# Three edits to a fused adaLN, attention and FFN kernel: VectorE's last residual ahead of the pooling maxima, one activation-table set for Exp and Ln, and the third group's score rows behind half of the next keys

## The chip, the cores and the metric

The kernel runs on one core of a Trainium2 chip. The metric is the device time of one execution in microseconds; each kernel is run several times and the median is taken. The engines of the core are named as in the profile: PE is TensorE's matmul, PEld its weight load, DVE is VectorE, ACT is ScalarE, POOL is GpSimd, and SP is the engine that issues the DMAs.

## What is computed

The input `x` has 64 sequences of 64 tokens with 256 features. Cut to what matters:

```python
def reference(x, ...):
    # rotation of feature halves by an angle and a power that depend on the sequence
    a = amplitudes ** delta_t; ang = frequencies * delta_t
    c, s = a * cos(ang), a * sin(ang)
    xr = [c * x0 - s * x1, s * x0 + c * x1]
    # attention as a decaying recurrence, 16 heads of 16
    q, k, v = split(xr @ W_qkv.T); k = layernorm(k)
    S = sigmoid(log_gamma) * S + v k^T; y = S q
    x = x + y @ W_o.T
    # pooling: scores from tanh, masked softmax over the sequence, divided by a count
    scores = tanh(x @ W1 + b1) @ v
    p = softmax(where(mask, scores, NEG_INF))
    pooled = (p @ x) / cnt
    # FFN with fake quantisation: the scale is the largest |pooled| of the whole tensor
    xq = quant(pooled); h = quant(silu(xq @ Wg.T) * (xq @ Wu.T))
    return x + h @ Wd.T
```

The scale of `quant` needs the maximum over all of `pooled`, so no FFN product can start before the pooling of the last tokens is done.

## The kernel before

The 4096 tokens are worked on in eight groups of 512 (`G = 8`, index `g`). Every engine has its own program, written out by hand in order, and engines meet only at semaphores (`wait_ge`, `then_inc`), so an instruction that waits holds up all that stands behind it on its engine.

**Start.** SP loads the row of parameters. ScalarE makes the decays' logarithm from it (Abs, Exp, Ln: lines 688 to 690) and then the sines (693 to 696, semaphore `trig_ok`). VectorE reduces the angles (1478 to 1486, `ang_ok`), takes the mean of the key weights (1490 and 1491, `mean_ok`), multiplies sines by the powers (1497 and 1498, `cs1_ok`), and rotates group 0 with ScalarE's help (704 on ScalarE, 1505 on VectorE). GpSimd waits for `mean_ok`, centres the key weights (557), copies the other weights (560, 562), makes the remaining powers (543), makes tables (534 to 538, 615, 616), and then rotates group 1 (`rotate`, 575 to 583). GpSimd also makes the low part of every group's turned input (`low_x`, 589, semaphore `xl_ok`).

**A group on TensorE.** Scores of the first half of the heads, values projection (`project_v`), scores of the second half, then for `g` from 2 on the pooling network of group `g - 2` (`hidden_layer`, ScalarE's tanh, `score_rows`), then `values_pair` (the recurrence's values, which wait for VectorE's decays, `dec_done`), and between these the keys and queries of group `g + 1`. A projection of 128 rows is six matmuls of 512 columns; `project_half` issues the first three (step 0: lines 1136 to 1138) or the last three (step 1: 1140, 1142, 1143, of which the last two wait for `xl_ok`). `project_whole` issues both. In groups from 3 on, pooling matmuls stand between `hidden_layer` and `score_rows`; in the third group (`g = 2`) nothing does.

**The last group's tail.** TensorE projects the last output rows (`project`, line 978, `o_mm`), VectorE adds the residual in two halves (`residual(g, 0)` and `residual(g, 1)`, line 1571, `x1_done`), and TensorE's `pool_tokens(G - 1)` (line 1042) waits for both. VectorE further sums the softmax (1657 to 1663) and takes the maxima of group 6's pooled rows (1751, two reductions) and of group 7's (1759, two reductions), then of all (1762, `xm_ok`). TensorE spreads that maximum over the partitions (`every_row`, 1334), behind six matmuls that do no work of the reference (`keep_clock(6, ...)`, 1125), and the quantisation and the FFN follow. ScalarE meanwhile loads the table set for Silu and copies the pooled rows (`pooled_rows(6)`, `last_pooled_rows`, line 788).

Of the kernel before, what the change touches and what calls it, by code (L numbers as in the profile page):

```python
# [7 lines left out]
ALU = mybir.AluOpType  # L8
# [15 lines left out]
DC = D // P  # L24
# [3 lines left out]
PP = 4  # L28
TG = PP * P
G = TOK // TG  # L30
NPAIR = TOK // P
# [30 lines left out]
def build(nc, x, x_t, row, kinds, cols, w_qkv_t, w_o_t, w_o, w1, w_gate, w_up, w_down, out):  # L62
# [7 lines left out]
    with ExitStack() as ctx:  # L70
# [7 lines left out]
        bank = [psum[:, 512 * i:512 * i + 512] for i in range(8)]  # L78
# [124 lines left out]
        a_pow = sb("a_pow", [P, NPAIR])  # L203
        cs = sb("cs", [P, 2, NPAIR])
# [36 lines left out]
        x0_in, cs1_ok, csr_tr, csr_ok = sem("x0_in"), sem("cs1_ok"), sem("csr_tr"), sem("csr_ok")  # L241
# [436 lines left out]
        def _(act):  # L678
# [3 lines left out]
            def link(ins):  # L682
                count[0] += 1
                ins.then_inc(act_c, 1)
                act.wait_ge(act_c, count[0])

            act.wait_ge(ld_row, 16)
            link(act.activation(lg[:, 1, :], lg_raw, ACT.Abs))
            link(act.activation(lg[:, 2, :], lg[:, 1, :], ACT.Exp, scale=-1.0))
# [282 lines left out]
        def _(pe):  # L972
# [61 lines left out]
            def pool_tokens(c):  # L1034
                pe.wait_ge(pT_ok, c + 1)
                for q in range(2):
                    for e in range(2):
                        for b in range(2):
                            rows = slice(S * b, S * b + S)
                            weights = pT[c % 2][rows, q, e * S:e * S + S]  # L1040
                            if c >= TURNED:
                                last = pe.matmul(pool_out(c, q, b)[S * e:S * e + S, :], weights, x1[c % 3][rows, 2 * q + e, :],
                                                 start=True, stop=True)
                                continue
                            for k in range(DC):
                                at_p = k * TG // 2 + (2 * q + e) * S
                                last = pe.matmul(bank[b][:, at_p:at_p + S], x1[c % 3][rows, 2 * q + e, k * P:k * P + P], weights,
                                                 start=True, stop=True)
                    if c == G - 1 or q == 1:
                        last.then_inc(pl_mm, 1)  # L1050
# [159 lines left out]
            for g in range(G):  # L1210
                c = g - 2

                def project_whole(o, s, j, signal):
                    project_half(g + 1, o, s, j, 0, signal)
                    project_half(g + 1, o, s, j, 1, signal)
# [25 lines left out]
                if 3 <= g < G - 1:  # L1241
                    pe.wait_ge(v_ok, PP * g + PP)
                    pool_tokens(c - 1)
                if 2 <= g < G - 1:
                    score_rows(c)
                if g + 1 < G:
# [13 lines left out]
                    if g != 1:  # L1260
                        pe.wait_ge(xT_ok, DC * (g + 1) + DC)
                        pe.wait_ge(v_ok, PP * g + PP)
                        if g >= 3:
                            pe.wait_ge(pl_cp, 2 * c - 1)
                        project_whole(K_BANK, 1, 0, k_mm)
                        if g >= 3:
                            pe.wait_ge(pl_cp, 2 * c)
                        project_whole(K_BANK, 1, 1, k_mm)
# [182 lines left out]
        def _(dve):  # L1451
# [33 lines left out]
            link(dve.tensor_tensor(ang[:, 3, :], ang[:, 3, :], ang[:, 2, :], ALU.min))  # L1485
            dve.tensor_scalar(ang[:, 3, :], ang[:, 3, :], np.pi / 2, None, ALU.add).then_inc(ang_ok, 1)

            dve.wait_ge(ld_k, 16)
            raw_heads = raw_qkv[:, :, D:2 * D].rearrange("p c (h d) -> p c h d", d=DK)
            link(dve.tensor_reduce(mean[:, :, :], raw_heads, AX.X, ALU.add))  # L1490
            dve.tensor_scalar(mean[:, :, :], mean[:, :, :], 1.0 / DK, None, ALU.mult).then_inc(mean_ok, 1)


            first, rest = slice(0, 2 * PP), slice(2 * PP, NPAIR)
            dve.wait_ge(pow_ok, 1)
            dve.wait_ge(trig_ok, 2)
            dve.tensor_tensor(cs[:, 1, first], a_pow[:, first], bank[2][:, first], ALU.mult)
            dve.tensor_tensor(cs[:, 0, first], a_pow[:, first], bank[3][:, first], ALU.mult).then_inc(cs1_ok, 1)
            dve.wait_ge(cs1_ok, 1)
            dve.wait_ge(x0_in, 16)  # L1500
            for h, sign in enumerate((ALU.subtract, ALU.add)):
# [64 lines left out]
            def residual(g, h):  # L1566
                dve.wait_ge(o_mm, 2 * g + h + 1)
                if h == 0:
                    dve.wait_ge(xres_in, 16 * g + 16)
                two = slice(2 * h, 2 * h + 2)  # L1570
                dve.tensor_tensor(x1[g % 3][:, two, :], o_bank(g, h).rearrange("q (p d) -> q p d", p=2), xres[:, two, :],
                                  ALU.add).then_inc(x1_done, 1)
# [82 lines left out]
            def softmax_sums(c):  # L1655
                dve.wait_ge(ex_ok, c + 1)
                dve.tensor_reduce(sm_c[:, 1, :], ex[:, :, :], AX.X, ALU.add).then_inc(cond_c, 1)
# [19 lines left out]
            for g in range(G):  # L1677
# [65 lines left out]
                if g + 1 < G:  # L1743
                    newton(g + 1, 1 if g else None)
                residual(g, 0)
                if g == G - 1:
                    softmax_sums(g)
                    softmax_weights(g)
                    dve.wait_ge(pl_mm, G - 1)
                    for b in range(2):  # L1750
                        dve.tensor_reduce(raw_max[:, 0, :].rearrange("p (q b) -> p b q", b=2)[:, b, :], bank[b].rearrange("p (q d) -> p q d", d=D), AX.X,
                                          ALU.max, apply_absolute_value=True).then_inc(pl_ok, 1)
                residual(g, 1)

            c = G - 1
            for q in range(2):
# [177 lines left out]
```

## Time and profile before

| what | value |
|---|---|
| median of 3 runs | 263.94 us (263.81 to 265.27) |
| the profiled execution's own time | 265.14 us |
| its span in the profile | 263.4 us |
| mean granted TensorE clock | 0.994 of full speed |
| TensorE, VectorE, ScalarE, GpSimd busy | 94%, 84%, 72%, 62% of the span |

All stretches below are read from the one profiled execution, whose own time is 1.74 us more than its span. Times inside it are counted from the span's start. The rows themselves stand in groups further below.

### The profile page before, as it was taken

What the parts mean: (1) busy time and instruction counts of PE and PEld (TensorE: products, weight loads), DVE (VectorE), ACT (ScalarE), POOL (GpSimd) and SP (SyncE); (2) the same over time, 40 slices, a digit from 0 to 9 for tenths busy, and PEclk for the clock granted to TensorE, in tenths of its full rate; (3) what the DMA queues carried; (4) which work ended last, traced back from release to release, by engine and by line L of the source; (5) the groups of instructions that cost most, each with busy time, mean ns of one, the idle gap of its engine ahead of it and who ended that gap; (6) DMA issues with size and microseconds to landing.
All of it is one profiled execution on the core that took longest, in us unless ns stands there. A gap on an engine that the chain in (4) does not pass through costs nothing.

```text
span 263.4 us, 8405 instructions
## 1 busy us (share of the span) xinstructions
PE 247.8 (94%) x3476; PEld 170.4 (65%) x3481; DVE 220.2 (84%) x481; ACT 189.0 (72%) x327; POOL 163.2 (62%) x170
## 2 busy tenths in 40 slices
PE   4999999998999999999999999996899999998994
PEld 4779688696798788789679668765334444443331
DVE  4879679789789889689879849969579999999994
ACT  5895464772796798598694683384699899919990
POOL 6898583796697696694894925240043689730670
PEclk9999999999999999999999999999799999999999
DMA  5991406808607508907906620310056797000367
GB/s 163 341 298 31 150 2 212 113 2 278 122 6 276 124 2 274 188 4 244 207 17 184 121 82 3 113 50 4 0 138 142 129 256 296 0 2 0 118 247 274
DMA packets 42983, 34.34 MB, mean 130 GB/s; under 512 B 25601, under 2 KB 33345, under 8 KB 42945
## 3 DMA queue, kind: packets, MB, share of 16 engines
q1 hardware_dynamic: 42944, 33.80, 47.3%
q8 instruction: 27, 0.44, 0.7%
q14 instruction: 12, 0.09, 0.1%
HBM read 19.48 MB, written 8.42 MB: 106 GB/s over the span
## 4 chain that ended last, share of the span: by engine, by line
PE 71%; DVE 11%; ACT 11%; issue 4%; DMA 1%; POOL 1%; DVEq 0%; ACTq 0%
PE psum L978 17%; PE psum L1017 7%; PE psum L1002 7%; PE psum L1389 6%; PE psum L1136 4%; PE psum L1408 4%; PE psum L1125 3%; DVE arena L1563 3%; PE psum L1142 3%; PE psum L1143 2%; ACT silu L941 2%; PE psum L1140 2%; PE psum L1083 2%; PE psum L1137 2%; PE psum L1138 2%
## 5 line engine op out<-in xcount | busy, mean ns | idle before, releaser
L1563 DVE TENSOR_TENSOR arena<-psum,xq_mem 128x512 f32<-128x512 f32 x64 | 39.7, 683 | 2.2 <-PE psum L1002 2.1
L1389 PE MATMUL psum<-xq_mem,guT 128*128 128x512 bf16 x151 | 33.8, 380 | 0.3
L589 POOL TENSOR_TENSOR xT_lo<-arena,xT 128x512 fp32r<-128x512 f32 x14 | 17.6, 1276 | 16.2 <-ACT xT L739 16.2
L1389 PEld LDWEIGHTS psum<-xq_mem,guT 128*128 128x128 bf16 x152 | 14.4, 98 | 19.3 <-DVE arena L1787 1.8
L1798 DVE TENSOR_REDUCE h_max<-arena 128x1 f32<-128x1024 f32 (+1 forms) x24 | 25.9, 1122 | 0.2
L923 ACT ACTIVATE silu<-psum,gu_x 128x1024 f32<-128x1024 f32 (+1 forms) x24 | 24.4, 1026 | 2.1 <-PE psum L1389 1.1
L721 ACT ACTIVATE arena<-psum,pmask 128x512 f32<-128x512 f32 x32 | 20.2, 686 | 0.8 <-PE psum L1143 0.6
L1017 PE MATMUL psum<-arena 64*32 64x128 f32 x1024 | 19.1, 274 | 1.3 <-DVE arena L1563 1.3
L1408 PE MATMUL psum<-arena,dT 128*128 128x512 bf16 x78 | 18.8, 380 | 1.3 <-DVE arena L1857 0.6
L1002 PE MATMUL psum<-arena 32*64 32x128 f32 x1024 | 19.7, 278 | 0.0
L1017 PEld LDWEIGHTS psum<-arena 64*32 64x32 f32 x1024 | 13.8, 105 | 7.2 <-issue 7.2
L664 POOL CAST arena<-silu 128x1024 bf16<-128x1024 int8 (+1 forms) x9 | 9.6, 1096 | 14.3 <-DVE silu L1852 13.1
L647 POOL CAST arena<-q 128x1024 bf16<-128x1024 int8 x6 | 6.2, 1039 | 18.8 <-ACT q L905 18.8
L575 POOL TENSOR_TENSOR arena<-xin,cs_rows 128x512 f32<-128x512 f32 x7 | 9.0, 1288 | 14.1 <-DMA cs_rows<-cs_dram 14.1
L978 PE MATMUL psum<-wT,xT 128*128 128x256 f32 x64 | 17.5, 295 | 0.0
L1578 DVE SCALAR_TENSOR_TENSOR psum<-psum,pmask,arena 128x256 f32<-128x256 f32 x28 | 12.4, 488 | 6.0 <-ACT arena L728 6.0
L1002 PEld LDWEIGHTS psum<-arena 32*64 32x64 f32 x1024 | 15.6, 130 | 2.7 <-issue 0.5
L978 PE MATMUL psum<-woT,yT 128*128 128x256 f32 x64 | 17.1, 289 | 0.2 <-DVE arena L1652 0.2
L715 ACT ACTIVATE arena<-psum 128x512 f32<-128x512 f32 x16 | 9.6, 599 | 10.5 <-PE psum L1143 10.5
L624 POOL COPY arena<-arena 128x512 uint16<-128x512 uint16 x24 | 16.9, 775 | 0.0
L978 PE MATMUL psum<-wT_lo,xT 128*128 128x256 f32 x64 | 16.7, 283 | 0.0
L978 PE MATMUL psum<-woT_lo,yT 128*128 128x256 f32 x64 | 16.7, 283 | 0.0
(250 smaller groups left out, 725.7 us busy)
## 6 DMA issues: line engine op xcount, KB each, us to landing
arena<-in_x SPq DMA_DIRECT2D x9, 512.0 KB, 4.4
x_dram<-arena SPq DMA_DIRECT2D x8, 512.0 KB, 3.1
pooled<-x_dram SPq DMA_DIRECT2D x8, 512.0 KB, 5.5
out<-pooled SPq DMA_DIRECT2D x15, 256.0 KB, 2.1
xin<-in_x_t SPq DMA_DIRECT2D x7, 512.0 KB, 5.7
cs_rows<-cs_dram SPq DMA_DIRECT2D x12, 256.0 KB, 5.5
pooled<-in_w_qkv_t SPq DMA_DIRECT2D x3, 256.0 KB, 5.3
pooled<-in_w_down SPq DMA_DIRECT2D x1, 704.0 KB, 8.4
```

The source lines that it names most:

```text
L589: pool.tensor_tensor(xT_lo[:, k, :], xrotT[:, k, :], xT[:, k, :].bitcast(F32), ALU.subtract).then_inc(xl_ok, 1)
L624: last = pool.tensor_copy(x1T_words[:, a, h], planesT[:, a, h])
L721: act.activation(qblk[:, c, odd, :], Q_BANK[c][:, :], ACT.Identity, scale=pmask[:, odd:odd + 1]).then_inc(q_ok, 1)
L923: act.activation(silu_tile(n, v)[:, a:], gate_bank(v)[:, a:], ACT.Silu, scale=gu_x[:, 0, v:v + 1]).then_inc(silu_ok, 1)
L978: return pe.matmul(o, w(k), x(k), start=start, stop=stop) if stationary_w else pe.matmul(o, x(k), w(k), start=start, stop=stop)
L1002: mm = pe.matmul(bank[S_BANK[r]][S * b:S * b + S, p * P:p * P + P], kT[rows, c, t:t + S], qblk[rows, c, :, t:t + S], start=True, stop=True)
L1017: last = pe.matmul(Y_BANK[half][b][32 * r:32 * r + 32, at_y:at_y + P], v_rows[rows, p, at_v:at_v + 32], dec[rows, c, r, p, :], start=True, ...
L1389: mm = pe.matmul(in_order(o[:, 512 * half:512 * half + 512], 2 * n + half), gT[i][:, v, c, :], xq_rows(2 * n + half, c), start=(c == 0), s ...
L1408: return pe.matmul(o, dT[:, c, v, :], hid_q[:, U * n + 2 * v + half, 0:512], start=first, stop=last)
L1563: dve.tensor_tensor(dec[:, c, r, :, :], bank[S_BANK[r]].rearrange("q (n k) -> q n k", n=PP), two_heads, ALU.mult).then_inc(dec_done, 1)
L1578: dve.scalar_tensor_tensor(o, y_psum(b, half, 1), pmask[:, 1:2], y_rows(b, half), ALU.mult, ALU.add).then_inc(y_ok, 1)
L1798: dve.tensor_reduce(h_max[:, n, v:v + 1], hid_step(n, v), AX.X, ALU.max, apply_absolute_value=True).then_inc(hm_done, 1)
```

## The change

Four things move. ScalarE is told at its start to load the table set `natural_log_exp_and_others`, which holds Exp and Ln, so no load stands between the two any more. VectorE multiplies the sines before it takes the mean of the key weights. In the third group, TensorE issues the first three matmuls of the next keys ahead of the score rows instead of behind the first `values_pair`. In the last group VectorE adds the second residual right behind the first, then takes group 6's maxima, and only then does the softmax sums.

```diff
--- before.py
+++ after.py
@@ -684,6 +684,7 @@
                 ins.then_inc(act_c, 1)
                 act.wait_ge(act_c, count[0])
 
+            act.preload_act_table_set("natural_log_exp_and_others")
             act.wait_ge(ld_row, 16)
             link(act.activation(lg[:, 1, :], lg_raw, ACT.Abs))
             link(act.activation(lg[:, 2, :], lg[:, 1, :], ACT.Exp, scale=-1.0))
@@ -1241,6 +1242,10 @@
                 if 3 <= g < G - 1:
                     pe.wait_ge(v_ok, PP * g + PP)
                     pool_tokens(c - 1)
+                if g == 2:
+                    pe.wait_ge(xT_ok, DC * (g + 1) + DC)
+                    pe.wait_ge(v_ok, PP * g + PP)
+                    project_half(g + 1, K_BANK, 1, 0, 0, k_mm)
                 if 2 <= g < G - 1:
                     score_rows(c)
                 if g + 1 < G:
@@ -1262,7 +1267,9 @@
                         pe.wait_ge(v_ok, PP * g + PP)
                         if g >= 3:
                             pe.wait_ge(pl_cp, 2 * c - 1)
-                        project_whole(K_BANK, 1, 0, k_mm)
+                        if g != 2:
+                            project_half(g + 1, K_BANK, 1, 0, 0, k_mm)
+                        project_half(g + 1, K_BANK, 1, 0, 1, k_mm)
                         if g >= 3:
                             pe.wait_ge(pl_cp, 2 * c)
                         project_whole(K_BANK, 1, 1, k_mm)
@@ -1485,17 +1492,18 @@
             link(dve.tensor_tensor(ang[:, 3, :], ang[:, 3, :], ang[:, 2, :], ALU.min))
             dve.tensor_scalar(ang[:, 3, :], ang[:, 3, :], np.pi / 2, None, ALU.add).then_inc(ang_ok, 1)
 
-            dve.wait_ge(ld_k, 16)
-            raw_heads = raw_qkv[:, :, D:2 * D].rearrange("p c (h d) -> p c h d", d=DK)
-            link(dve.tensor_reduce(mean[:, :, :], raw_heads, AX.X, ALU.add))
-            dve.tensor_scalar(mean[:, :, :], mean[:, :, :], 1.0 / DK, None, ALU.mult).then_inc(mean_ok, 1)
-
-
             first, rest = slice(0, 2 * PP), slice(2 * PP, NPAIR)
             dve.wait_ge(pow_ok, 1)
             dve.wait_ge(trig_ok, 2)
             dve.tensor_tensor(cs[:, 1, first], a_pow[:, first], bank[2][:, first], ALU.mult)
             dve.tensor_tensor(cs[:, 0, first], a_pow[:, first], bank[3][:, first], ALU.mult).then_inc(cs1_ok, 1)
+
+            dve.wait_ge(ld_k, 16)
+            raw_heads = raw_qkv[:, :, D:2 * D].rearrange("p c (h d) -> p c h d", d=DK)
+            link(dve.tensor_reduce(mean[:, :, :], raw_heads, AX.X, ALU.add))
+            dve.tensor_scalar(mean[:, :, :], mean[:, :, :], 1.0 / DK, None, ALU.mult).then_inc(mean_ok, 1)
+
+
             dve.wait_ge(cs1_ok, 1)
             dve.wait_ge(x0_in, 16)
             for h, sign in enumerate((ALU.subtract, ALU.add)):
@@ -1743,14 +1751,14 @@
                 if g + 1 < G:
                     newton(g + 1, 1 if g else None)
                 residual(g, 0)
+                residual(g, 1)
                 if g == G - 1:
-                    softmax_sums(g)
-                    softmax_weights(g)
                     dve.wait_ge(pl_mm, G - 1)
                     for b in range(2):
                         dve.tensor_reduce(raw_max[:, 0, :].rearrange("p (q b) -> p b q", b=2)[:, b, :], bank[b].rearrange("p (q d) -> p q d", d=D), AX.X,
                                           ALU.max, apply_absolute_value=True).then_inc(pl_ok, 1)
-                residual(g, 1)
+                    softmax_sums(g)
+                    softmax_weights(g)
 
             c = G - 1
             for q in range(2):
```

VectorE's order at the start of the program. `ang` are the angles, `mean` the key weights' means, `cs` the products of power and sine, and `arena` receives the rotated group 0. Before:

```order
L1486 TENSOR_SCALAR ang<-ang 128x32
L1490 TENSOR_REDUCE mean<-pooled 128x32
L1491 TENSOR_SCALAR mean<-mean 128x32
L1497 TENSOR_TENSOR cs<-a_pow,psum 128x8
L1498 TENSOR_TENSOR cs<-a_pow,psum 128x8
L1505 SCALAR_TENSOR_TENSOR arena<-arena,cs,psum 128x128 x8
```

Now:

```order
L1493 TENSOR_SCALAR ang<-ang 128x32
L1498 TENSOR_TENSOR cs<-a_pow,psum 128x8
L1499 TENSOR_TENSOR cs<-a_pow,psum 128x8
L1503 TENSOR_REDUCE mean<-pooled 128x32
L1504 TENSOR_SCALAR mean<-mean 128x32
L1513 SCALAR_TENSOR_TENSOR arena<-arena,cs,psum 128x128 x8
```

The two multiplications have passed the reduction and its scaling.

TensorE's order in the third group, from `hidden_layer` (`w_sb`) over the score rows (`v_rep`) and the first `values_pair` (32x128) to the end of the first projection of keys. Before:

```order
L1083 MATMUL psum<-arena,w_sb 64x256 x4
L1118 MATMUL psum<-arena,v_rep 64x128 x4
L1017 MATMUL psum<-arena 32x128 x16
L1136 MATMUL psum<-xT,wT 128x512
L1137 MATMUL psum<-xT,wT_lo 128x512
L1138 MATMUL psum<-xT,wT 128x512
L1140 MATMUL psum<-xT,wT_lo 128x512
L1142 MATMUL psum<-xT_lo,wT 128x512
L1143 MATMUL psum<-xT_lo,wT 128x512
```

Now:

```order
L1084 MATMUL psum<-arena,w_sb 64x256 x4
L1137 MATMUL psum<-xT,wT 128x512
L1138 MATMUL psum<-xT,wT_lo 128x512
L1139 MATMUL psum<-xT,wT 128x512
L1119 MATMUL psum<-arena,v_rep 64x128 x4
L1018 MATMUL psum<-arena 32x128 x16
L1141 MATMUL psum<-xT,wT_lo 128x512
L1143 MATMUL psum<-xT_lo,wT 128x512
L1144 MATMUL psum<-xT_lo,wT 128x512
```

Three matmuls have moved ahead of the score rows and the values; nothing was added.

VectorE's order in the last group's tail (`arena<-psum,arena` is a residual, `sm_c` and `inv_sum` the softmax sums, `raw_max` the maxima). Before:

```order
L1571 TENSOR_TENSOR arena<-psum,arena 128x512
L1657 TENSOR_REDUCE sm_c<-arena 128x4
L1661 TENSOR_TENSOR sm_c<-sm_c,cnt 128x4
L1663 RECIPROCAL inv_sum<-sm_c 128x4
L1751 TENSOR_REDUCE raw_max<-psum 128x2 x2
L1571 TENSOR_TENSOR arena<-psum,arena 128x512
L1759 TENSOR_REDUCE raw_max<-psum 128x2 x2
```

Now:

```order
L1579 TENSOR_TENSOR arena<-psum,arena 128x512 x2
L1758 TENSOR_REDUCE raw_max<-psum 128x2 x2
L1665 TENSOR_REDUCE sm_c<-arena 128x4
L1669 TENSOR_TENSOR sm_c<-sm_c,cnt 128x4
L1671 RECIPROCAL inv_sum<-sm_c 128x4
L1767 TENSOR_REDUCE raw_max<-psum 128x2 x2
```

The second residual has passed five instructions; the same seven kinds of work remain.

## Rows read from the trace of the kernel before

**Rows 1.** The page's first part: busy time, share of the span, instructions.

```profile
PE 247.8 (94%) x3476; PEld 170.4 (65%) x3481; DVE 220.2 (84%) x481; ACT 189.0 (72%) x327; POOL 163.2 (62%) x170
```

**Rows 2.** Timeline, start of the program: start us, us, engine, line, operation.

```profile
4.60 1.28 ACT L690 ACT_TABLE_LOAD   x1
...
6.13 1.28 ACT L693 ACT_TABLE_LOAD   x1
...
6.57 0.20 DVE L1486 TENSOR_SCALAR ang<-ang 128x32 f32<-128x32 f32 x1
6.68 0.67 DVE L1490 TENSOR_REDUCE mean<-pooled 128x32 f32<-128x512 f32 x1
...
7.39 0.18 DVE L1491 TENSOR_SCALAR mean<-mean 128x32 f32<-128x32 f32 x1
7.43 0.18 ACT L693 ACTIVATE psum<-ang 128x8 f32<-128x8 f32 x1
...
7.75 1.06 POOL L557 TENSOR_TENSOR arena<-pooled,mean 128x512 f32<-128x512 f32 x1 [0.64 <-DVE mean L1491]
...
7.80 0.16 DVE L1497 TENSOR_TENSOR cs<-a_pow,psum 128x8 f32<-128x8 f32 x1 [0.23 <-ACT psum L694]
...
8.65 2.27 DVE L1505 SCALAR_TENSOR_TENSOR arena<-arena,cs,psum 128x128 f32<-128x128 f32 x8 [0.61 <-ACT psum L704]
```

**Rows 3.** Timeline, group 0: GpSimd's low parts and TensorE's first use.

```profile
25.44 2.50 POOL L589 TENSOR_TENSOR xT_lo<-arena,xT 128x512 fp32r<-128x512 f32 x2 [0.74 <-ACT xT L739]
...
29.14 0.40 PE L1142 MATMUL psum<-xT_lo,wT 128*128 128x512 f32 x1
```

**Rows 4.** Timeline, third group (g = 2), TensorE.

```profile
64.07 0.66 PE L1118 MATMUL psum<-arena,v_rep 128*64 128x128 f32 x8 [0.67 <-ACT arena L762]
...
65.01 0.67 PE L1017 MATMUL psum<-arena 64*32 64x128 f32 x32 [0.28 <-DVE arena L1563]
...
65.61 0.50 PE L1136 MATMUL psum<-xT,wT 128*128 128x512 f32 x1
...
66.42 0.40 PE L1140 MATMUL psum<-xT,wT_lo 128*128 128x512 f32 x1
```

**Rows 5.** Timeline, last group's tail.

```profile
181.21 0.68 DVE L1571 TENSOR_TENSOR arena<-psum,arena 128x512 f32<-128x512 f32 x1
...
181.74 0.40 PE L978 MATMUL psum<-woT,yT_lo 128*128 128x256 f32 x2
181.81 0.41 DVE L1657 TENSOR_REDUCE sm_c<-arena 128x4 f32<-128x256 f32 x1
...
182.66 1.29 DVE L1751 TENSOR_REDUCE raw_max<-psum 128x2 f32<-128x512 f32 x2
...
183.86 0.68 DVE L1571 TENSOR_TENSOR arena<-psum,arena 128x512 f32<-128x512 f32 x1
...
184.20 1.55 ACT L788 ACTIVATE pooled<-psum,inv_sum 128x256 f32<-128x256 f32 x4
...
184.60 1.76 PE L1042 MATMUL psum<-arena 64*64 64x256 f32 x16 [2.24 <-DVE arena L1571]
...
186.41 0.69 DVE L1759 TENSOR_REDUCE raw_max<-psum 128x2 f32<-128x512 f32 x1 [0.16 <-PE psum L1042]
186.70 2.04 PE L1125 MATMUL psum<-guT 128*128 128x512 bf16 x5 [0.33 <-issue]
...
187.34 0.17 DVE L1762 TENSOR_REDUCE x_sc<-p_max 128x1 f32<-128x14 f32 x1
...
188.57 0.27 PE L1334 MATMUL psum<-ident,x_sc 128*128 128x128 f32 x1
```

**Rows 6.** Busy time, granted clock (PEclk) by stretch around the tail.

```profile
182.00:184.60 2.60, 0.36 (x5) 0.12 (x3) 2.44 (x6) 2.17 (x5) 0.00 (x0) 1.00 0.03 6
184.60:186.40 1.80, 1.76 (x16) 0.82 (x18) 0.69 (x1) 1.27 (x5) 0.00 (x0) 0.58 0.00 0
...
188.60:190.70 2.10, 1.34 (x11) 0.90 (x10) 1.68 (x6) 1.10 (x2) 0.00 (x0) 1.00 0.00 0
```

## The prediction

> **What bounds the kernel now.** I read the busy times first: TensorE works for 94% of the span [rows 1], so what counts is what TensorE waits for or runs slowly. The chain of work that ended last agrees: it goes through ScalarE and VectorE for the first 11 us, then almost wholly through TensorE until the last group, then in turns through ScalarE, VectorE and TensorE until the FFN. The waits of TensorE then show three places, and each edit lies at one of them.
>
> At the start ScalarE goes through two table loads of 1.28 us, from 4.60 and from 6.13, and the first sine starts at 7.43 [rows 2]. VectorE had the angles at 6.57 + 0.20 = 6.77 [rows 2], so for 0.66 us only the load was missing. The product with the powers starts at 7.80 and the rotation at 8.65 [rows 2].
>
> In the third group TensorE stands 0.67 us before the score rows, for ScalarE's tanh, and 0.28 us before the values, for VectorE's decays [rows 4].
>
> In the last group TensorE stands 2.24 us, for VectorE's second residual at 183.86 [rows 5]. Its input was complete much earlier: the last projection ends at 181.74 + 0.40 = 182.14 [rows 5]. Right behind this stretch TensorE's granted clock is low: 1.00 of full speed while it waited, 0.58 on average over the 1.80 us after it [rows 6], so mostly the 1.2 GHz level, and back at 1.00 by 188.60 [rows 6].
>
> **The start.** The second load goes away and Ln follows Exp. ScalarE then has Ln where the load was, at 4.60, and the sines' load begins 6.13 - 5.88 = 0.25 later as it does behind Ln today, at about 4.85, and ends at 6.13: before the angles, so that VectorE's 6.77 decides. With 0.07 for the semaphore the sine starts at 6.84, that is 0.59 earlier than 7.43 [rows 2]. The product starts 0.37 after the sine today (7.80 against 7.43), so at 7.21.
>
> Had VectorE kept its order, the mean would still have ended at 7.39 + 0.18 = 7.57 [rows 2] and eaten most of that. Now it comes behind: the second product is issued 0.08 after the first, the reduction follows at about 7.38, takes 0.67, and its scaling starts at 8.08 and ends at 8.26. What queues behind it is the rotation, ready at 8.65 - 0.59 = 8.06 but begun at about 8.19. Its eight pieces take 2.27 us [rows 2] and are paced by ScalarE's equal pieces, so a late begin is mostly caught up; I take 0.48 us earlier for its end, between 0.46 and 0.59.
>
> The mean is 8.26 - 7.57 = 0.69 later for GpSimd, which waited for it already (0.64 idle before line 557) [rows 2] and then works without a gap up to group 1's rotation. So group 1's rotation, ScalarE's copy of it and GpSimd's low parts are 0.69 later: their end goes from 25.44 + 2.50 = 27.94 to 28.63 [rows 3]. TensorE uses them at 29.14 [rows 3]; with 0.06 for the semaphore it can begin at 28.69, so at most 0.45 earlier than today. The start therefore is worth 0.45 us (0.3 to 0.59 as bounds), and GpSimd takes over there as what is late next. Later GpSimd waits for ScalarE again in every group, so the lateness is not carried on.
>
> A rule of the Trainium skill stands against this term. By "ScalarE: Activation LUTs", section "What ACT_TABLE_LOAD costs", a switch costs the load and a drain, about 2.66 us together. With that the sines' table would be ready only at about 4.82 + 2.66 = 7.48, no earlier than today's sine, and the sum would be 0.45 us smaller. The trace disagrees: Ln and the sine follow directly on loads of 1.28 us [rows 2], so the sum goes by the rows.
>
> **The third group.** The three matmuls of keys need only the turned input and the bank that VectorE has emptied before its decays, both there by then. They take 66.42 - 65.61 = 0.81 us [rows 4]. The gap before the score rows is 0.67 (plus the end of the matmul before), so the score rows move by about 0.05 us at most, and the 0.28 us of waiting for VectorE behind them [rows 4] hides that. The values stay at 65.01, and behind them three matmuls are missing. A projection's first matmul after another kind takes 0.1 us more (0.50 against 0.40 [rows 4]), which line 1140 now pays: gain 0.70 us, bounds 0.5 and 0.81. ScalarE's square and copy of these keys stand behind the exponentials of the same group and could start about 0.7 us earlier too, which just fits. If it did not, squares of the keys would be late next.
>
> **The last group's tail.** VectorE's first residual is issued at 181.21 and the next instruction 0.60 later; the second residual waits for TensorE's 182.14 and starts at about 182.20, today 183.86 [rows 5]. It ends at about 182.86, and TensorE's pooling starts at 182.92 instead of 184.60, which is 1.68 us. The transposed weights are there by about 182.8. What the move delays is group 6's maxima and the softmax sums on VectorE, and who waits for those is ScalarE (pooled rows of group 6) and the whole maximum. ScalarE loads Silu's table until 184.1 and begins at 184.20 [rows 5]; the maxima are there by 184.1, so it stays covered.
>
> VectorE's work, with pitches from today's starts: residual 0.60, group 6's maxima 183.86 - 182.66 = 1.20, sums 182.66 - 181.81 = 0.85, group 7's two maxima 1.20, then 187.34 - 186.41 = 0.93 to line 1762 and 0.17 for it [rows 5]. From 182.20 that gives 182.20 + 0.60 + 1.20 + 0.85 + 0.60 = 185.45 for the last maximum's start and 185.45 + 0.93 + 0.17 = 186.55 for the end, against 187.51 today. But today TensorE takes this up only at 188.57 [rows 5]: it is still in its six idle matmuls, of which five recorded ones take 2.04 us at the lower clock. Now it has finished them earlier. At the full clock the pooling takes about 1.76 x 0.58 = 1.02 us and the six about 2.04 / 5 x 6 / 2 = 1.2, with 0.33 between: 182.92 + 1.02 + 0.33 + 1.2 = 185.5, before 186.55. So line 1334 starts at 186.61, and the gain is 1.96 us. If the clock fell all the same, TensorE would decide, and the gain is the plain shift of 1.68. ScalarE's eight pooled rows end at about 184.20 + 8 x 0.39 = 187.3, and the scale is ready at about 187.6, 0.3 us of cover.
>
> **Sum.** 0.45 + 0.70 + 1.96 = 3.11 us. Against the profiled execution that is 265.14 - 3.1 = 262.0 (span 260.3). The median of before is 1.20 us lower than that execution, so the forecast for the median is 263.94 - 3.11 = 260.8 us.
>
> **Rivals.** (a) The clock holds in the pooling but falls later. TensorE now waits about 1 us before line 1334, and then works in small pieces up to the FFN: today that later stretch was 1.34 of 2.10 us busy at 1.00 [rows 6], while 0.36 of 2.60 us busy was followed by the fall. The two together are in between, so it can't be read off. Price: a low stretch of at most 4.0 us (today's lies between 184.60 and 188.60), in which matmuls double, so at most 2.0 us and less where ScalarE sets the pace: 261.3 to 262.8 us. The Trainium skill, "TensorE: Matmul & The Clock Gate", section "Loop structure matters more than you think", says the same in general: waits between matmuls make the engine cold. 17 in 100.
>
> (b) One of the two small terms is nothing: GpSimd's rotation is later than I think, or ScalarE holds up the keys of the third group. 260.83 + 0.45 = 261.3 or 260.83 + 0.70 = 261.5 us. 13 in 100.
>
> (c) The tail does not do what it says: another wait (ScalarE's copies or the transposed weights) is right behind the residual, and only about 0.5 us is left of 1.96: 262.3 us or somewhat more, no change to be told. For it speaks only how near ScalarE's cover is. 5 in 100.
>
> (d) Slower: the clock at 1.2 GHz well into the FFN, where TensorE is bound. Each us there costs half a us, so the gain is used up after 6.2 us and 0.5% is lost after 8.8 us, for 265.3 us or more. Today's low stretch is less than half as long. 3 in 100.
>
> My forecast has the remaining 62 in 100, with 260.3 to 261.2 as its own range from the terms' bounds (largest sum 0.59 + 0.81 + 1.96 = 3.36) and some noise. To leave out no more than 2 in 10 the range reaches through (b) and most of (a): 260.0 to 262.3 us. A measurement of this kernel tells about 0.5%, 1.3 us, from no change. Faster by more than that, below 262.6: 0.92; within it, from (c) and the far end of (a): 0.05; slower: 0.03.
>
> **What the profile would show.** Right: the first sine at about 6.84 and the product at 7.2; no wait before the score rows in the third group and values still behind VectorE; TensorE's wait before the last pooling 0.6 us with clock 1.00 behind it, sixteen matmuls in about 1.1 us, and a new wait of about 1 us before line 1334. Wrong: a sine still at 7.4, a wait of over 0.3 us for low parts at the keys of group 1, a clock under 1.00 between 183 and 192 us, or an FFN longer than before.

## The result, and the profile after

The changed kernel takes 262.46 us (median of 20 runs, 262.06 to 264.82), the kernel before 264.72 us in the same comparison (20 runs, 263.67 to 265.34). The ratio is 0.9926, with a 95% interval of 0.9911 to 0.9941: about 1.96 us faster (the two medians differ by 2.26). The forecast was 260.8 us, 1.2% faster, with a range of 260.0 to 262.3. The direction was right, the size was not: 262.46 lies outside the range.

The first lines of the page of after, against a span of 263.4 us and [rows 1] before:

```profile
span 260.7 us, 8410 instructions
...
PE 247.4 (95%) x3481; PEld 170.1 (65%) x3481; DVE 220.8 (85%) x481; ACT 187.6 (72%) x326; POOL 163.5 (63%) x170
```

The span is 2.7 us shorter, near the forecast's 3.1, while the comparison of many runs gives 1.96 from a median of before that is 264.72 and not 263.94. Where these numbers part is the main finding, below.

The timeline of after at the start of the program (start us, us, engine, line, operation) answers to [rows 2]:

```profile
4.84 1.28 ACT L694 ACT_TABLE_LOAD   x1
...
6.56 0.20 DVE L1493 TENSOR_SCALAR ang<-ang 128x32 f32<-128x32 f32 x1
6.79 0.18 ACT L694 ACTIVATE psum<-ang 128x8 f32<-128x8 f32 x1 [0.67 <-DVE ang L1493]
...
7.17 0.16 DVE L1498 TENSOR_TENSOR cs<-a_pow,psum 128x8 f32<-128x8 f32 x1 [0.41 <-ACT psum L695]
...
8.16 2.16 DVE L1513 SCALAR_TENSOR_TENSOR arena<-arena,cs,psum 128x128 f32<-128x128 f32 x8
8.39 1.06 POOL L557 TENSOR_TENSOR arena<-pooled,mean 128x512 f32<-128x512 f32 x1 [1.29 <-DVE mean L1504]
```

The sines' table is loaded from 4.84, the sine waits for the angles and starts at 6.79, the product at 7.17, the rotation at 8.16: each within 0.05 us of the forecast. Group 0 answers to [rows 3]:

```profile
25.54 2.96 POOL L589 TENSOR_TENSOR xT_lo<-arena,xT 128x512 fp32r<-128x512 f32 x2 [0.74 <-ACT xT L740]
...
28.55 0.19 PEld L1143 LDWEIGHTS psum<-xT_lo,wT 128*128 128x128 f32 x1 [0.30 <-POOL xT_lo L589]
28.56 0.50 PE L1143 MATMUL psum<-xT_lo,wT 128*128 128x512 f32 x1
```

GpSimd's low parts end at 28.50, and TensorE takes them at 28.56, 0.58 us earlier than before, right behind their end: its weight load stood 0.30 us for them, just at the limit that the prediction set for this wait.

The third group of after answers to [rows 4]; GpSimd's and VectorE's rows are shown as well:

```profile
60.00 0.74 POOL L610 TENSOR_TENSOR xq_mem<-xq_mem 128x256 f32<-128x256 f32 x1
...
60.09 0.68 DVE L1563 TENSOR_SCALAR g_sc<-g_sc 128x6 f32<-128x6 f32 x1
...
63.74 0.66 PE L1119 MATMUL psum<-arena,v_rep 128*64 128x128 f32 x8
...
64.84 0.67 PE L1018 MATMUL psum<-arena 64*32 64x128 f32 x32 [0.44 <-DVE arena L1571]
...
65.44 0.50 PE L1141 MATMUL psum<-xT,wT_lo 128*128 128x512 f32 x1
```

There is no wait left before the score rows (63.74), but 0.44 us before the values (64.84) instead of 0.28. VectorE's scaling of 6 columns took 0.68 us and ended at 60.77, just when GpSimd's operation ended (60.00 + 0.74).

The tail of after answers to [rows 5]:

```profile
180.41 0.68 DVE L1579 TENSOR_TENSOR arena<-psum,arena 128x512 f32<-128x512 f32 x1
...
181.38 0.69 DVE L1579 TENSOR_TENSOR arena<-psum,arena 128x512 f32<-128x512 f32 x1 [0.29 <-PE psum L979]
...
182.12 1.09 PE L1043 MATMUL psum<-arena 64*64 64x256 f32 x16 [0.56 <-DVE arena L1579]
...
183.15 1.47 PE L1126 MATMUL psum<-guT 128*128 128x512 bf16 x6
...
183.40 3.01 ACT L789 ACTIVATE pooled<-psum,inv_sum 128x256 f32<-128x256 f32 x8
...
184.03 1.29 DVE L1767 TENSOR_REDUCE raw_max<-psum 128x2 f32<-128x512 f32 x2
...
185.56 0.17 DVE L1770 TENSOR_REDUCE x_sc<-p_max 128x1 f32<-128x14 f32 x1
...
185.78 0.32 PE L1341 MATMUL psum<-ident,x_sc 128*128 128x128 f32 x1 [1.16 <-DVE x_sc L1770]
```

And the stretches around it answer to [rows 6] (length, busy time and count of PE, PEld, DVE, ACT and POOL, granted clock, DMA share, GB/s):

```profile
181.00:183.40 2.40, 1.83 (x23) 0.97 (x23) 2.11 (x5) 1.77 (x3) 0.00 (x0) 1.00 0.00 0
183.40:185.00 1.60, 1.22 (x6) 0.37 (x4) 1.50 (x5) 1.60 (x6) 0.00 (x0) 1.00 0.00 0
185.00:187.00 2.00, 0.88 (x6) 0.65 (x7) 1.41 (x7) 1.55 (x5) 0.00 (x0) 1.00 0.00 0
187.00:190.00 3.00, 2.15 (x11) 0.93 (x12) 2.60 (x7) 3.00 (x4) 0.28 (x1) 1.00 0.01 3
```

The pooling starts at 182.12, the wait before it is down from 2.24 to 0.56 us, and the clock is 1.00 throughout. The new wait before line 1341 (the old 1334) is 1.16 us.

### The profile page after: what moved, and what is told of

Read it like the earlier page. It is cut to its first block, busy times and chain, and to the rows that moved or that the text cites. A ratio compares the mean times of both kernels' runs of the same rounds, so it can differ in the third digit from the quotient of the medians.

```text
span 260.7 us, 8410 instructions
## 1 busy us (share of the span) xinstructions
PE 247.4 (95%) x3481; PEld 170.1 (65%) x3481; DVE 220.8 (85%) x481; ACT 187.6 (72%) x326; POOL 163.5 (63%) x170
## 4 chain that ended last, share of the span: by engine, by line
PE 70%; DVE 13%; ACT 10%; issue 5%; POOL 1%; DVEq 0%; POOLq 0%; ACTq 0%
PE psum L979 17%; PE psum L1018 7%; PE psum L1003 6%; PE psum L1126 4%; DVE arena L1571 4%; PE psum L1415 4%; PE psum L1137 4%; ACT silu L924 3%; PE psum L1143 3%; DVE arena L1795 3%; PE psum L1144 2%; PE psum L1141 2%; ACT silu L942 2%; PE psum L1396 2%; PE psum L1084 2%
## 5 line engine op out<-in xcount | busy, mean ns | idle before, releaser
L746 ACT ACTIVATE arena<-arena 128x1024 uint16<-128x1024 uint16 x12 | 12.0, 1045 | 6.2 <-DVE arena L1579 6.2
```

## The experiments

Every execution comes with its mean granted clock. Sorted by it, executions of before fall into two heaps without overlap in that number: 0.999 and more, where the clock held, and 0.993 to 0.994, where it fell somewhere for a few us. The other kernels' executions show 0.997 and more, or 0.993 to 0.994. "Clock held" and "clock fell" below mean these; the mean does not tell where in the execution the clock fell, only the traces do. Medians in us, number of executions in brackets; the columns of before are those of the same comparison (for the changed kernel's own, no clocks of before are listed).

| kernel | clock held | before, held | clock fell | before, fell |
|---|---|---|---|---|
| changed kernel | 262.34 (14) | | 263.27 (6) | |
| tail_only | 263.35 (10) | 263.80 (17) | 264.12 (2) | 265.16 (18) |
| gap_filled | 263.77 (12) | 263.80 | none | 265.16 |
| no_tail | 262.81 (10) | 263.80 | 264.53 (2) | 265.16 |
| before_again | 263.91 (7) | 263.80 | 265.14 (5) | 265.16 |
| start_only | 263.65 (4) | 263.72 (11) | 264.61 (8) | 265.24 (12) |
| third_only | 263.13 (5) | 263.72 | 264.36 (7) | 265.24 |
| scales_later | 262.27 (4) | 263.72 | 262.91 (2) | 265.24 |
| idle_filled | 262.24 (6) | 263.72 | none | 265.24 |
| all_scales_later | 261.94 (1) | 263.75 (11) | 262.94 (5) | 265.08 (12) |
| scales_and_fill | 262.04 (6) | 263.75 | none | 265.08 |
| preload_only | 263.44 (4) | 263.75 | 264.74 (8) | 265.08 |
| mean_only | 263.95 (7) | 263.75 | 265.25 (5) | 265.08 |

### The tail, and the two levels of before

**tail_only**: before, with only VectorE's new order in the last group.

```diff
                 residual(g, 0)
+                residual(g, 1)
                 if g == G - 1:
-                    softmax_sums(g)
-                    softmax_weights(g)
                     dve.wait_ge(pl_mm, G - 1)
...
-                residual(g, 1)
+                    softmax_sums(g)
+                    softmax_weights(g)
```

> Only VectorE's new order in the last group. Theory A (two levels of before are one event: TensorE's granted clock falls to 1.2 GHz behind the 2.24 us wait in some executions and not in others): the tail is worth 1.96 us against executions whose clock fell and only about 0.7 us against those whose clock held, so the median gain is 0.7 to 2.0 us by the mixture, about 1.4 us, and the profile shows TensorE's last pooling 1.68 us earlier with clock 1.00 behind it. Theory B (the tail is worth a fixed 1.96 us and the rest of the change loses something): a gain of 1.9 to 2.0 us against the median, whatever the clock.

Measured: 263.36 us against 264.40, ratio 0.9964 (0.9946 to 0.9982). In its trace line 1334 starts at 186.59 against 188.57 [rows 5], 1.98 us earlier and within 0.02 of the forecast's 1.96, in a profile of before in which the clock fell. Executions with the clock held gained only 0.45 us, those with the clock fallen 1.04; from the fallen heap of before to the held one of this kernel it is 1.81 us (265.16 - 263.35), near the forecast. Theory A holds, with less in the first heap than its 0.7, and theory B does not.

**before_again**: the kernel before, unchanged.

> The kernel before once more, for the granted clock of each single execution. Theory A: executions near 263.9 us show a mean granted clock of 0.998 to 1.0 and those near 265.2 us one near 0.994. Theory B: clock and level do not go together. No difference in the median.

Measured: 263.98 us, ratio 0.9996 (0.9975 to 1.0017). Clock and level go together in all 93 executions of before listed with a clock, in the three comparisons and here: 46 with the clock held between 263.56 and 264.12, 47 with it fallen between 264.40 and 265.51. Its trace is of an execution in which the clock fell: the pooling takes 1.96 us, and line 1334 starts 3.97 us behind the pooling's start (188.64 against 184.67), the same spacing as in [rows 5].

**gap_filled**: before, with eight idle matmuls in the 2.24 us wait.

```diff
             weights_turn(G - 1)
-            pe.wait_ge(x1_done, 2 * G)
-            pool_tokens(G - 1)
             pe.wait_ge(gT_in[0], 16)
             pe.wait_ge(gT_in[1], 16)
+            keep_clock(8, bank[6], gT_flat[0][:, 0:P], gT_flat[0][:, 0:512])
+            pe.wait_ge(x1_done, 2 * G)
+            pool_tokens(G - 1)
```

> The kernel before, with eight idle matmuls of 512 columns put into TensorE's 2.24 us wait ahead of the last pooling; nothing else moves and VectorE's order is the old one. Theory A: the clock holds in every execution, the pooling takes 1.1 us instead of 1.76, the spread of the maximum starts 1.1 to 1.3 us earlier where the clock fell before, so all times lie within about 0.4 us around 263.9 and the upper level near 265.2 is gone; the median gains 0.6 to 1.1 us. Theory B (the two levels come from elsewhere, such as the transfers at the start): both levels, 1.3 us apart, are still there and the median does not move.

Measured: 263.77 us, ratio 0.9982 (0.9966 to 0.9998), all 12 executions with the clock held and between 263.66 and 264.11. TensorE's timeline, to be read against [rows 5]:

```profile
182.37 1.89 PE L1125 MATMUL psum<-guT 128*128 128x512 bf16 x8
184.78 1.09 PE L1042 MATMUL psum<-arena 64*64 64x256 f32 x16 [0.52 <-DVE arena L1572]
185.81 1.47 PE L1125 MATMUL psum<-guT 128*128 128x512 bf16 x6
187.26 0.32 PE L1335 MATMUL psum<-ident,x_sc 128*128 128x128 f32 x1
```

The pooling takes 1.09 us instead of 1.76 and line 1334 (here 1335) follows 2.48 us behind its start instead of 3.97. The same spacing, within 0.01 us, is in an execution of third_only in which the clock held with the wait unfilled; VectorE's rows stand with it:

```profile
180.68 0.68 DVE L1577 TENSOR_TENSOR arena<-psum,arena 128x512 f32<-128x512 f32 x1
...
184.07 1.09 PE L1042 MATMUL psum<-arena 64*64 64x256 f32 x16 [2.24 <-DVE arena L1577]
184.80 1.29 DVE L1765 TENSOR_REDUCE raw_max<-psum 128x2 f32<-128x512 f32 x2 [0.79 <-PE psum L1042]
...
185.32 1.24 PE L1125 MATMUL psum<-guT 128*128 128x512 bf16 x5 [0.16 <-issue]
...
186.32 0.17 DVE L1768 TENSOR_REDUCE x_sc<-p_max 128x1 f32<-128x14 f32 x1
...
186.54 0.32 PE L1340 MATMUL psum<-ident,x_sc 128*128 128x128 f32 x1
```

In the same comparison 18 of 35 executions of before had the clock fallen, and 0 of 12 here. So the wait of 2.24 us is what the fall hangs on, and the fall costs 3.97 - 2.48 = 1.5 us, which is about the distance of the heaps (265.16 - 263.80 = 1.36). What decides in which executions the clock falls behind the same wait, no run shows.

The rows of third_only also show why so little of the tail is left where the clock held. There TensorE takes the maximum as soon as VectorE has it (186.32 + 0.17, then 186.54), as it does in after. So what counts is VectorE's own stretch from its first residual to line 1768 (1770 in after): 186.32 - 180.68 = 5.64 us in third_only and 185.56 - 180.41 = 5.15 in after. VectorE does the same work in both; what differs is its waiting, 0.79 us for the pooling's result in third_only and 0.29 us for the second residual's input in after. So 0.5 us is left of the 1.68 by which the pooling starts earlier.

**no_tail**: the changed kernel with VectorE's old order in the tail (the reverse of the diff of tail_only).

> The changed kernel with VectorE's old order in the last group, so the start and the third group alone. The changed kernel's trace gives these two 0.80 to 0.85 us by the score rows of group 3 (forecast was 1.15). Expected by both theories: 0.8 us faster, two levels 1.3 us apart as before. Should it be 1.15 us, the shortfall would lie in the tail instead.

Measured: 262.96 us, ratio 0.9955 (0.9934 to 0.9977); 0.99 us with the clock held, between the 0.8 and the 1.15 of the expectation. In its trace the score rows of group 3 are 1.11 us earlier than before, not 0.85 as in the changed kernel: there VectorE's small scaling took 0.33 us instead of 0.68. The same code gives different gains from one execution to the next.

### The start and the third group, one at a time

**start_only**: before, with the table set loaded ahead and the mean behind the products (the first and fourth piece of the change's diff).

> The kernel before with the table set loaded ahead and the means behind the products; third group and tail as before. Among executions of equal clock: 0.45 us faster by the forecast, 0.49 by the changed kernel's trace at the third group's second scores. Rival: the start's gain is swallowed at the third group, where VectorE's scaling of 6 columns waits for GpSimd, and only 0.1 to 0.2 us reaches the end.

Measured: 264.52 us, ratio 0.9985 (0.9965 to 1.0004). In its trace everything from the third group to the tail is 0.50 to 0.53 us earlier. With the clock fallen it gains 0.63 us (8 executions), with it held 0.07 (4), and no_tail less third_only, which is the start once more, gives 0.99 - 0.59 = 0.40 with it held. So few executions do not settle the size; I go by the trace, and why the held heap shows so little stays open.

**third_only**: before, with only the three matmuls moved (the second and third piece).

> The kernel before with only the three matmuls of the next keys moved ahead of the third group's score rows. Among executions of equal clock 0.70 us faster by the forecast. If the shortfall of the changed kernel (0.36 instead of 0.70 here) comes only from VectorE's phase against GpSimd after an earlier start, this kernel has the old phase and gains the full 0.6 to 0.7 us with the values still at 65.0 us. If the estimate of the three matmuls is itself too large, it gains 0.4.

Measured: 264.12 us, ratio 0.9979 (0.9956 to 1.0001); 0.59 us with the clock held. Third group, all engines:

```profile
60.25 0.74 POOL L610 TENSOR_TENSOR xq_mem<-xq_mem 128x256 f32<-128x256 f32 x1
...
60.50 0.51 DVE L1561 TENSOR_SCALAR g_sc<-g_sc 128x6 f32<-128x6 f32 x1
...
65.08 0.67 PE L1017 MATMUL psum<-arena 64*32 64x128 f32 x32 [0.27 <-DVE arena L1569]
...
65.69 0.50 PE L1140 MATMUL psum<-xT,wT_lo 128*128 128x512 f32 x1
```

The score rows of group 3 are 0.57 us earlier than before. The three matmuls are worth what was forecast: line 1140 starts 65.69 - 65.08 = 0.61 behind the values as line 1136 did before (0.60), and the 0.81 us in front of it [rows 4] are gone, less 0.07 by which the values are later (65.08 against 65.01), less 0.1 for the longer first matmul; 0.07 of the rest stays open. Even here the scaling took 0.51 us instead of 0.16. The expectation of an undisturbed phase was wrong. The kernel before is not free of it either; in the trace of before_again stands

```profile
60.24 0.74 POOL L610 TENSOR_TENSOR xq_mem<-xq_mem 128x256 f32<-128x256 f32 x1
...
60.55 0.46 DVE L1555 TENSOR_SCALAR g_sc<-g_sc 128x6 f32<-128x6 f32 x1
```

and its values start at 65.08 as well. Against that execution third_only's score rows of group 3 are 0.64 us earlier (85.10 against 85.74), nearly the forecast's 0.70. The 65.01 of [rows 4] comes from an execution in which the scaling happened not to be held up.

**preload_only** and **mean_only**: the two halves of the start.

> The kernel before with only the table set loaded ahead. By the forecast's working the sine is ready at 6.84, but VectorE's mean still ends at 7.57, so the product starts at about 7.5 instead of 7.80 and about 0.3 us of the start's 0.59 are left at the rotation; 0.2 to 0.3 us at the end, at equal clock. Rival (the load is what counts and the mean is hidden): 0.5 us.

> The kernel before with only the mean behind the products. The products wait for the sine at 7.7 as before, since the mean was ready by 7.57, and the mean, now behind them, ends about 1.2 us later; the rotation's first piece starts behind it, and GpSimd gets the mean at about 8.8. Expected: no gain, 0 to 0.2 us slower, and GpSimd's rotation of group 1 later by 0.2 to 1 us. Rival (the order alone gives the start's gain): 0.4 us faster.

Measured: preload_only 264.58 us, ratio 0.9987 (0.9966 to 1.0009), 0.31 to 0.34 us better at equal clock. mean_only 264.06 us, ratio 1.0005 (0.9982 to 1.0028), 0.17 to 0.20 us worse at equal clock. Timeline of preload_only:

```profile
6.78 0.18 ACT L694 ACTIVATE psum<-ang 128x8 f32<-128x8 f32 x1 [0.67 <-DVE ang L1487]
...
7.37 0.18 DVE L1492 TENSOR_SCALAR mean<-mean 128x32 f32<-128x32 f32 x1
7.46 0.15 DVE L1498 TENSOR_TENSOR cs<-a_pow,psum 128x8 f32<-128x8 f32 x1
```

The sine is there at 6.78, but the product waits for the mean until 7.46. Timeline of mean_only:

```profile
7.80 0.16 DVE L1491 TENSOR_TENSOR cs<-a_pow,psum 128x8 f32<-128x8 f32 x1 [1.04 <-ACT psum L694]
...
9.02 1.06 POOL L557 TENSOR_TENSOR arena<-pooled,mean 128x512 f32<-128x512 f32 x1 [1.92 <-DVE mean L1497]
```

The product still waits for the sine (7.80), and the mean comes late for VectorE and for GpSimd (9.02 against 7.75 [rows 2]). By these traces neither edit is worth the start's gain alone: the third group's score rows are 0.38 us earlier in preload_only (63.69), 0.14 later in mean_only (64.21) and 0.52 earlier in start_only (63.55). In the times the difference between start_only and preload_only is not settled (0.63 against 0.34 us with the clock fallen, 0.07 against 0.31 with it held).

### The scaling that waits for GpSimd

**scales_later**: the changed kernel, third group's scaling behind the decays.

```diff
-                if 2 <= g < 4:
+                if g == 3:
                     scales(g - 2, ...)
...
                 decays(g, 1)
+                if g == 2:
+                    scales(0, g_sc[:, 0, :], g_inv[:, 0, :], g_sc_ok[0])
```

> The changed kernel with the third group's two operations of 6 columns (scales of the gate weights) moved behind VectorE's second decays. Theory: in the changed kernel the first of them takes 0.68 us instead of 0.16 because it waits for GpSimd's operation to end, and the decays and TensorE's values behind it come late. Without them ahead, the decays start right after the values' scaling, TensorE's wait of 0.44 us before the values falls to under 0.1, and the kernel is 0.3 to 0.4 us faster than the changed one (262.0 us at the full clock). Rival (the decays wait for TensorE's scores and not for those two): no difference.

Measured: 262.61 us, ratio 0.992 (0.9891 to 0.995). In its trace the values start at 64.51 instead of 64.84, so the place is right and 0.33 us is won there. At the end it is not to be seen: 262.27 against 262.34 with the clock held, where 0.3 to 0.4 us were expected. This execution took 263.27 us, and the timeline of its next group shows where it went:

```profile
80.89 2.58 POOL L589 TENSOR_TENSOR xT_lo<-arena,xT 128x512 fp32r<-128x512 f32 x2
81.04 1.24 DVE L1563 TENSOR_SCALAR g_sc<-g_sc 128x6 f32<-128x6 f32 x1
...
83.86 2.05 PE L1048 MATMUL psum<-arena 64*128 64x64 f32 x32 [1.18 <-DVE arena L1648]
```

The scaling that was left in group 3 took 1.24 us under GpSimd's operation, the decays and the pooling matmuls came late, and TensorE stood 1.18 us where it had not stood in after. Two of VectorE's operations shortly ahead of it, each with two inputs in SBUF, were long too: 0.66 us instead of 0.17 for 4 columns (at 79.39, ending 0.02 us behind GpSimd's operation) and 0.82 instead of 0.42 for 256. In this execution a gain won by moving one operation was lost at the next.

**all_scales_later**: the same for the groups 2, 3 and 4.

> The changed kernel with VectorE's small scaling operations of the groups 2, 3 and 4 all moved behind the second decays of their group. Theory: in some executions such an operation ahead of the values' scaling waits out a GpSimd operation (up to 1.24 us instead of 0.16 in the group 3 of one execution) and the decays come late, which makes the outliers of the changed kernel and of the last experiment (263 us and more at the full clock). With all three out of that place, the executions at the full clock lie closer together (within 0.5 us instead of 0.9) and their median is 0.1 to 0.3 us lower than 262.34. Rival (the small operations only pass the wait on to the next one): median and spread as before.

Measured: 262.93 us, ratio 0.9931 (0.9905 to 0.9957). Five of six executions had the clock fallen, so the heaps are too small to say what the move is worth; one at 261.94 with the clock held is the only hint. Neither theory is settled. The profile caught a fall of the new kind, by windows:

```profile
186.00:187.00 1.00, 0.66 (x5) 0.42 (x4) 0.90 (x4) 0.63 (x2) 0.00 (x0) 1.00 0.00 0
187.00:188.00 1.00, 0.58 (x3) 0.28 (x3) 0.80 (x3) 1.00 (x2) 0.00 (x0) 0.70 0.00 0
188.00:189.00 1.00, 1.00 (x4) 0.24 (x2) 0.84 (x2) 1.00 (x2) 0.00 (x0) 0.50 0.00 0
189.00:190.00 1.00, 1.00 (x4) 0.33 (x4) 1.00 (x3) 0.74 (x2) 0.77 (x1) 0.50 0.00 0
190.00:192.00 2.00, 2.00 (x9) 0.86 (x8) 1.34 (x3) 1.78 (x3) 0.27 (x1) 0.80 0.51 175
```

The pooling and the six idle matmuls ran at 1.00; the clock fell at about 187.4, behind the 1.16 us wait and the small pieces of work after it, and the first FFN matmuls ran at 1.2 GHz until about 190.8 (2.00 us at 0.80 on average, from 0.50 to 1.00). This is the forecast's rival (a).

### Filling the new wait

**idle_filled**: the changed kernel with 11 idle matmuls instead of 6.

```diff
-            keep_clock(6, bank[6], gT_flat[0][:, 0:P], gT_flat[0][:, 0:512])
+            keep_clock(11, bank[6], gT_flat[0][:, 0:P], gT_flat[0][:, 0:512])
```

> The changed kernel with 11 idle matmuls instead of 6 ahead of the spread of the maximum, so TensorE's wait of 1.16 us there is filled to about 0.1. Theory: the executions of the changed kernel with a mean clock of 0.993 (6 of 20, about 0.9 us slower) have their fall in or behind that wait; here they vanish or get much rarer, the level at the full clock stays at 262.3 us, and the spread of the maximum starts at the same 185.8 us. Rival (the fall comes at another place, or from the 0.56 us wait before the pooling): 2 to 4 of 12 executions still show 0.993.

Measured: 262.24 us, ratio 0.9915 (0.9889 to 0.9941), six executions, all with the clock held. TensorE's timeline:

```profile
182.99 2.32 PE L1126 MATMUL psum<-guT 128*128 128x512 bf16 x10 [0.16 <-issue]
185.40 0.32 PE L1341 MATMUL psum<-ident,x_sc 128*128 128x128 f32 x1
```

The spread follows the idle matmuls without a wait and is no later for it: it starts 3.66 us behind the pooling (181.74), as in after. The level with the clock held is 262.24 against 262.34.

**scales_and_fill**: idle_filled and all_scales_later together.

> Both ideas on the changed kernel: all three scalings behind the decays, and 11 idle matmuls ahead of the spread of the maximum. If both theories hold: no execution with a mean clock of 0.993, all within 0.5 us, median 262.0 to 262.2 us, which is below both kernels. If only the clock's holds: as with the 11 idle matmuls alone, 262.24.

Measured: 262.04 us, ratio 0.9908 (0.9883 to 0.9933), all six with the clock held, but one at 262.86, so the spread did not shrink as expected. Its median is the lowest of all kernels, 0.4 us below the changed one; the intervals overlap, and only the clock's part is shown, by the two kernels with 11 idle matmuls together. In the kernels with VectorE's new tail and six idle matmuls the clock fell in 15 of 44 executions, in the two with 11 in 0 of 12.

## Why the prediction was wrong

**The failed step** is the last of the sum: "The median of before is 1.20 us lower than that execution, so the forecast for the median is 263.94 - 3.11 = 260.8 us." The 1.20 us is no constant between a profile and a median. The profiled execution was one with the clock fallen; the median of the three runs, 263.94, lies at the level of those with it held (the clocks of these three runs are not listed). The tail's 1.96 us contains the 1.5 us that the fall cost, and I took them off a run that had not paid them. With the clock held the tail is worth 3.97 - 3.66 + 1.68 - 1.5 = 0.49 us (line 1334 comes 3.66 us behind the pooling's start in after, 2.48 before); VectorE's stretch says 5.64 - 5.15 = 0.49, and the heaps of tail_only say 0.45. The 20 runs of before, whose median is 264.72, are by their times a mixture of both heaps, 8 at 264.00 or less and 12 at 264.54 or more; the first three were two of the one and one of the other. With the clock held on both sides the whole change is worth about 1.4 us (263.7 to 263.8 against 262.34). [rows 6] showed the fall, and the three times (265.27, 263.81, 263.94) showed the levels; the two had to be put together.

**The start** was right in the traces: 0.49 us at the third group's second scores of after, 0.50 to 0.53 in start_only, forecast 0.45. GpSimd's rotation was not 0.69 us late but 0.10 (ScalarE's copy of group 1 at 24.83 instead of 24.73), since two small selects of GpSimd took 0.24 us each instead of 0.58. They came later, and VectorE's large operations had just ended there; that this is the reason is read from two traces and not tested. Its low parts took 2.96 us instead of 2.50, so TensorE took them right at their end: the limit that I named was there, by another path, and that it came out near 0.45 is in part luck. The Trainium skill's rule on the drain, 2.66 us for a switch ("ScalarE: Activation LUTs", section "What ACT_TABLE_LOAD costs"), does not hold at this place: by it the table would be ready at 4.84 + 2.66 = 7.50, and the sine started at 6.79, right behind the angles.

**The third group** was mis-sized: 0.36 us more after it than before it in the changed kernel, forecast 0.70. The matmuls were costed rightly. What failed is "The values stay at 65.01": counted with the start's gain they should have come 0.45 us earlier and came 0.17 earlier, since the scaling ahead of the decays was held up beside GpSimd's operation. In no_tail, with a shorter such wait, the two terms together gave 1.11 of the forecast 1.15. The wait is no product of the change: it is in before_again too (0.46 us), and the profile of before was an execution without it. How much of the missing 0.34 us (0.70 - 0.36) comes from this wait is not shown.

**The tail** was right as long as the clock had fallen before: 1.68 us for the pooling, 1.99 for the spread of the maximum beyond what the first two terms gave there (2.79 - 0.80), forecast 1.96. ScalarE's cover held: its eight copies end at 186.41, the scale is ready later.

**The rivals.** (a) happened in 6 of 20 executions and costs 0.93 us (263.27 against 262.34), less than its upper bound. (b) came half true for the third group. (c) came true in size and not in mechanism: about 0.5 us is left of the tail where the clock held, but what stands right behind the second residual is VectorE's own work, and neither ScalarE's copies nor the weights. (d) did not happen. Put right, the sum for the median of executions with the clock held is 263.8 - 0.49 - 0.36 - 0.49 = 262.5 us, and 262.34 was measured; that sum is made of readings from after, so it explains and does not test.

## What to carry to other kernels

Before a sum made in one profiled execution is taken off a median, look whether the execution and the median are of the same kind: here the mean granted clock of every run (0.994 or 1.00) told them apart, and a gain that consists of a fall of the clock counts only in the runs that fall. When a long wait of TensorE is closed, look for the next light stretch behind it: the clock can fall there, and idle matmuls that fill it cost nothing while the engine waits anyway. When one engine is let off early, ask which engine's own work is then the longest stretch: here it was VectorE's. An operation of a few columns ahead of a critical one is not cheap if GpSimd has begun an operation beside it.

## What the runs showed of the hardware

With the same wait of 2.24 us in the program, TensorE's clock fell in 47 of 93 executions of the kernel before and held in 46, and fell in 30 of 60 of the five other kernels with VectorE's old tail and the wait unfilled; with waits of 0.56 and 1.16 us and light work behind them, it fell in 15 of 44. The Trainium skill, "TensorE: Matmul & The Clock Gate", section "What's actually happening", says that the number of slow matmuls at a kernel's start varies from run to run; these runs show the same of a wait in the middle of a kernel, where the outcome is worth 0.9 to 1.5 us.

VectorE's scaling of 6 columns, both sides in SBUF, took 0.16 or 0.17 us in the third group of five traces (before, tail_only, start_only, preload_only and idle_filled), and in each of these it began before GpSimd's operation of line 610, in tail_only by only 0.03 us. In six traces it began while that operation ran and took 0.33 (no_tail), 0.46 (before_again), 0.51 (third_only), 0.56 (gap_filled), 0.63 (mean_only) and 0.68 us (after), and ended 0.02 to 0.04 us behind it in all six. The reciprocal of the same 6 columns took 0.19 us beside the same GpSimd operation (start_only, 60.25, with GpSimd's from 60.15). The Trainium skill, "GPSIMD Engine Reference", section "8. Key points", says that GpSimd shares its SBUF interfaces with VectorE, with contention for VectorE's operations in a 2-port mode or with two SBUF inputs; the traces fit this, and show that the scaling waits out the rest of the GpSimd operation if that began first. No run here took GpSimd's operation away, so the cause rests on these coincidences in time.
